# Fifteen tiles of each edge loop fetched row by row through SyncE's queue instead of gathered by GpSimd

## What is computed

```python
def layer0(x, src, dst, edge_attr, u, W1, b1, W2, b2):      # batch is all zeros
    all_feat = concatenate([x[dst], x[src], edge_attr, u[0] for each edge])
    msg = relu(all_feat @ W1 + b1)
    agg = segment_sum(msg, dst)
    return relu(concatenate([x, agg, u[0] for each node]) @ W2 + b2)
def layer1(h, fc_weight, attn_weight, src, dst, etype):
    Z = einsum('ni,rio->nro', h, fc_weight)                  # 8 relations
    z_s, z_d = Z[src, etype], Z[dst, etype]
    e = relu(sum(concatenate([z_s, z_d]) * attn_weight[etype]))
    alpha = softmax of e over the edges of each dst
    return segment_sum(alpha[:, None] * z_s, dst)
x = layernorm(x + layer0(...)); x = layernorm(x + layer1(...)); return x
```

## Time and profile before

| | |
|---|---|
| median of 3 runs | 4239.44 us |
| the profiled execution's own time | 4242.57 us |
| its span, first to last instruction | 4240.8 us |
| busy share of the span | PE 77%, PE weight loads 68%, DVE 70%, ACT 30%, POOL 72% |
| layer 0's gathers, on POOL | 36.1 to 1997.0 us |
| layer 1's gathers, on POOL | 2195.9 to 4156.1 us |
| mean granted TensorE clock | 0.519 |

### The profile page before, as it was taken

How to read it: one execution, slowest core, us unless ns; L and a number is a source line. 1 busy time by engine, 2 the same in 40 slices (tenths; PEclk the granted TensorE clock), 3 DMA queues, 4 the chain that set the end, 5 groups by cost and what they waited for, 6 DMA issues and landing times. The chain is left out here.

```text
span 4240.8 us, 71158 instructions
## 1 busy us (share of the span) xinstructions
PE 3261.1 (77%) x18045; PEld 2899.6 (68%) x18045; DVE 2980.9 (70%) x9475; ACT 1266.3 (30%) x4137; POOL 3036.0 (72%) x3266
## 2 busy tenths in 40 slices
PE   7867677777777777777857777787878888888884
PEld 6866666666676766767636666676767777777774
DVE  6867677777677777777446666676767777777777
ACT  3000000000000000000224545554555555555553
POOL 5777777777777777776147777777777777777774
PEclk7555555555555555555665555555555555555555
DMA  6322222222222222222352222222222222222221
GB/s 196 105 70 61 69 72 60 69 72 71 70 62 70 72 70 72 72 70 47 135 198 58 52 54 58 48 59 58 58 49 58 58 58 58 59 58 56 51 58 37
DMA packets 172567, 300.16 MB, mean 71 GB/s; under 512 B 71746, under 2 KB 78262, under 8 KB 158871
## 3 DMA queue, kind: packets, MB, share of 16 engines
q0 software_dynamic: 100032, 105.03, 14.8%
q1 hardware_dynamic: 70688, 188.26, 12.5%
q10 hardware_dynamic: 1462, 2.30, 0.2%
HBM read 260.37 MB, written 34.99 MB: 70 GB/s over the span
## 5 line engine op out<-in xcount | busy, mean ns | idle before, releaser
L451 POOL DMA_INDIRECT ring<-Btab,idx x1563 | 1484.7, 950 | 510.2 <-issue 443.7
L451 POOL DMA_INDIRECT ring<-Ztab,idx x1563 | 1485.2, 950 | 493.2 <-issue 449.5
L1312 PE MATMUL p_s<-ring,ohx 128*128 x3328 | 808.0, 421 | 122.7 <-issue 120.0
L1312 PEld LDWEIGHTS p_s<-ring,ohx 128*128 128x128 f32 x3328 | 735.8, 326 | 142.7 <-issue 142.7
L732 PEld LDWEIGHTS p_s<-msg,oh 128*128 128x128 f32 x3328 | 725.7, 331 | 101.8 <-issue 101.8
L732 PE MATMUL p_s<-msg,oh 128*128 128x64 f32 x3328 | 758.3, 423 | 47.4 <-ACT msg L632 44.1
L719 PE MATMUL p_m<-A,oht 128*128 x1664 | 436.7, 364 | 430.6 <-DVE full L853 423.0
L632 ACT ACTIVATE msg<-p_t 128x512 f32<-128x512 f32 x208 | 124.2, 597 | 1802.7 <-DVE p_t L859 1796.4
L719 PEld LDWEIGHTS p_m<-A,oht 128*128 128x128 bf16 x1664 | 234.6, 142 | 507.7 <-issue 462.3
L724 PE MATMUL p_m<-W1c,eaT 65*128 65x128 f32 x1664 | 572.6, 448 | 6.0 <-DMA eaT<-in_eaT_in 6.0
L1402 DVE SCALAR_TENSOR_TENSOR XA<-XA,ff,p_s 128x65 f32 x1664 | 467.5, 281 | 128.5 <-DVE XA L1402 70.5
(11 more groups left out here) (204 smaller groups left out, 3132.0 us busy)
## 6 DMA issues: line engine op xcount, KB each, us to landing
drow<-drow_d SPq DMA_DIRECT2D x104, 1024.0 KB
eaT<-in_eaT_in SPq DMA_DIRECT2D x208, 128.0 KB
Ztab<-Z_stage SPq DMA_DIRECT2D x49, 536.0 KB, 4.1
ring<-Btab,idx POOLq DMA_INDIRECT x1563
ring<-Ztab,idx POOLq DMA_INDIRECT x1563
xTB<-in_xTB_in SPq DMA_DIRECT2D x7, 448.0 KB, 7.0
Btab<-B_stage SPq DMA_DIRECT2D x7, 448.0 KB, 5.9
ring<-in_xTA_in SPq DMA_DIRECT2D x7, 448.0 KB, 6.3
```

Of the source, the lines that this page charges most:

```text
L451: e.indirect_dma_start(out=ring[:, t % RING, :], out_offset=None, in_=table[:, :], in_offset=bass.IndirectOffsetOnAxis(ap=idx[:, t:t + 1], ...
L1312: last = e.matmul(pS[s % 2][h][:, j % 4, :], OHx[:, s % 2, j, :], ring[:, bass.ds(t, 1), 0:D + 1], start=True, stop=True)
```

## The change

Of each edge loop, fifteen tiles are no longer gathered by POOL: the last tile of the super-tiles 17, 29, 41 and so on to 185 (`fetched_tile`). SP fetches each of them by 128 DMAs of one row each, eleven for each compute step, spread over twelve steps. It reads the row numbers from a small table in SBUF (`srow`), which it loads for one fetched tile ahead. The super-tiles that contain a fetched tile lie in 24 more places behind the ring (`place`). DVE works these places out in the input phase, with fifteen more small operations. POOL's `counted` waits for the fetched rows (`A.s_row`) beside the gathers of that super-tile. The tables of slot places lie in one SBUF tensor (`tabs`), so layer 1 does not load `xrow` a second time. In layer 1, SP waits for the phase's tables before it loads the first `drow`; before, two `drow` loads came ahead of that wait.

```diff
+W = 12
+SPARE = 3
+ROWS = -(-P // W)
+FIRST = W + 5
+NK = len(range(FIRST, TO - 1, W))
...
+            step, base = W * O, (FIRST - W) * O
+            done(e.tensor_scalar(out=lim[:, :, :], in0=A.iota[:, 0:16].unsqueeze(1), scalar1=float(step), scalar2=float(base), op0=ALU.mult, op1=ALU.add))
...
+            done(e.tensor_tensor(out=tm[:, :], in0=tm[:, :], in1=off[:, :], op=ALU.add))
+            for w in range(2):
+                done(e.tensor_copy(A.val[:, :, w, 2], tm[:, :]))
             e.wait_ge(s_pc, 1)
...
+def place(t):
...
+    s, j = divmod(t, O)
+    n, off = divmod(s - FIRST + W, W)
+    return RING + n % SPARE * O + j if off == 0 and n >= 0 else t % RING
...
+def fetched(e, A, s, ring, table, of, regs, used):
...
+    k, i = divmod(s, W)
+    if k >= NK:
+        return
+    t = fetched_tile(k)
+    if i == 0:
+        if k >= 2:
...
+            e.wait_ge(used, t // O - SPARE * W + BEHIND + 1)
+            e.wait_ge(A.s_row[k % 2], 16 * P * (k // 2))
+        e.wait_ge(A.s_srow, 16 * (k + 1))
+        if k + 1 < NK:
+            numbers(e, A, of, k + 1)
+    for p in range(i * ROWS, min((i + 1) * ROWS, P)):
+        if p % O == 0 or p == i * ROWS:
+            e.reg_load(regs, A.srow[0:1, k % 2 * P + p // O * O:k % 2 * P + p // O * O + O])
+        r = e.snap(regs[p % O], min_val=0, max_val=table.shape[0] - 1)
+        e.dma_start(ring[p:p + 1, place(t), :], table[bass.ds(r, 1), :]).then_inc(A.s_row[k % 2], 16)
...
-        e.indirect_dma_start(out=ring[:, t % RING, :], out_offset=None, in_=table[:, :],
-                             in_offset=bass.IndirectOffsetOnAxis(ap=idx[:, t:t + 1], axis=0)).then_inc(s_g[s % len(s_g)], 16)
+        if t not in others:
+            e.indirect_dma_start(out=ring[:, place(t), :], out_offset=None, in_=table[:, :],
+                                 in_offset=bass.IndirectOffsetOnAxis(ap=idx[:, t:t + 1], axis=0)).then_inc(s_g[s % len(s_g)], 16)
...
                     e.dma_start(eaT[0:2 * DE, s % QE, :, :], of[bass.ds(t, 1), :, :, :].rearrange("a f i k -> (a f) i k")).then_inc(s_ea[s % QE], 16)
+                    fetched(e, A, s, ring, A.Btab, src, regs, S["full"])
...
-            for g in range(SO // G):
-                rows_loaded(e, A, drow, s_dr, S["oht"], g)
-            e.wait_ge(s_ix, 80)
+            e.wait_ge(s_ix, 64)
+            numbers(e, A, A.ix1_d, 0)
+            regs = [e.alloc_register(f"l1sr{j}") for j in range(O)]
+            for s in range(SO):
+                if s % G == 0:
+                    rows_loaded(e, A, drow, s_dr, S["oht"], s // G)
+                fetched(e, A, s, ring, A.Ztab, A.ix1_d, regs, S["s"])
+            e.wait_ge(A.s_srow, 16 * NK)
```

More of the change, by code:

```diff
@@ L43 @@
 assert RT >= BEHIND + 5
+assert (SPARE - 1) * W > BEHIND and ROWS * W >= P and W > 6
 assert NS >= NT + NB - 1 and NS % P == 0 and TO % Q == 0 and SO % Q == 0 and SO % G == 0
@@ L129, in phase_inputs @@
         tm = sb("t_mod", [P, SC], F32)
+        lim = sb("t_lim", [P, 1, 16], F32)
+        ge = sb("t_ge", [P, SC, 16], F32)
+        tn = sb("t_n", [P, SC], F32)
+        off = sb("t_off", [P, SC], F32)
+        isn = sb("t_is", [P, SC], F32)
         pB = [[bank(ctx, nc, f"p_b{k}{h}", [P, QC, D]) for h in range(2)] for k in range(2)]
@@ L433, in weave, with fetched_tile, numbers @@
                 streams.remove(g)
+def place(t):
+    s, j = divmod(t, O)
+    n, off = divmod(s - FIRST + W, W)
+    return RING + n % SPARE * O + j if off == 0 and n >= 0 else t % RING
+def fetched_tile(k):
+    return (FIRST + k * W) * O + O - 1
+def numbers(e, A, of, k):
+    e.dma_start(A.srow[0:1, k % 2 * P:(k % 2 + 1) * P], of[:, fetched_tile(k):fetched_tile(k) + 1].rearrange("p c -> c p"),
+                allow_slow_non_contiguous=True).then_inc(A.s_srow, 16)
+def fetched(e, A, s, ring, table, of, regs, used):
[15 more added lines that the diff above has]
+        e.dma_start(ring[p:p + 1, place(t), :], table[bass.ds(r, 1), :]).then_inc(A.s_row[k % 2], 16)
 def gathers(e, A, ring, table, idx, s_g, landed, used, free={}):
+    others = {fetched_tile(k): k for k in range(NK)}
+    tiles = lambda s: sum(t < NT and t not in others for t in range(s * O, (s + 1) * O))
     def counted(s):
-        tiles = min(O, NT - s * O)
-        before = sum(min(O, NT - i * O) for i in range(s % len(s_g), s, len(s_g)))
-        e.wait_ge(s_g[s % len(s_g)], 16 * (before + tiles))
+        e.wait_ge(s_g[s % len(s_g)], 16 * sum(tiles(i) for i in range(s % len(s_g), s + 1, len(s_g))))
+        k = others.get(s * O + O - 1)
+        if k is not None:
+            e.wait_ge(A.s_row[k % 2], 16 * P * (k // 2 + 1))
         e.sem_inc(landed, 1)
@@ L524, in phase_layer0 @@
         s_io = sem("l0_io")
-        T = {n: sem("t_" + n) for n in ("dve count before middle low high typ val sq sel tab d0 rows rowt rowi back table dh dl lt yt ys "
-                                        "drow typd ixd ix a hi lo rem parts zero").split()}
+        T = {n: sem("t_" + n) for n in ("dve count before middle low high typ val sq sel tab d0 rows rowt rowi table dh dl lt yt ys "
+                                        "drow typd ix a hi lo rem parts zero").split()}
         block = ctx.enter_context(nc.Block())
@@ L531, in _ @@
             treg = e.alloc_register("l0st")
+            regs = [e.alloc_register(f"l0sr{j}") for j in range(O)]
             for i, (q0, q1) in enumerate(CHUNKS):
@@ L546, in _, with loads @@
             e.wait_ge(T["drow"], 16)
-            e.wait_ge(T["table"], 48)
+            e.wait_ge(T["table"], 64)
             rows_loaded(e, A, drow, s_dr, S["oht"], 0)
-            def loads(of):
+            def loads(of, src):
+                numbers(e, A, src, 0)
                 for s in range(SO):
@@ L1184, in _ @@
             e.wait_ge(A.s_x, 32)
+            for k in range(2):
+                take(e, A.s_row[k], 16 * P * len(range(k, NK, 2)))
+            take(e, A.s_srow, 16 * NK)
 def phase_layer1(nc, A):
@@ L1550, in build @@
         A.flag = sb("flag", [1, 1], I32)
-        A.brow = sb("brow", [1, NS], I32)
+        A.tabs = sb("tabs", [P, NS], I32)
+        A.brow = A.tabs[0:1, :]
+        A.wrow = A.tabs[32:33, :].rearrange("a (s j) -> a s j", j=O)
+        A.xrow = A.tabs[64:65, 0:SO * WX].rearrange("a (s w) -> a s w", w=WX)
+        A.srow = A.tabs[96:97, 0:2 * P]
+        A.s_row = [ctx.enter_context(nc.semaphore(f"rows_fetched{i}")) for i in range(2)]
+        A.s_srow = ctx.enter_context(nc.semaphore("row_numbers"))
         A.dstl = sb("dstl", [P, NS], BF16)
```

65 lines of the change are left out of this document (36 added, 29 removed).

## The result

| | before | after |
|---|---|---|
| median, same chip | 4239.44 us (4236.49 to 4252.38, 5 runs) | 4196.04 us (4194.93 to 4197.75, 5 runs) |
| profiled execution, its span | 4242.57, 4240.8 us | 4197.56, 4195.8 us |
| POOL busy | 3036.0 us | 3002.0 us |
| first gather to last, layer 0 | 1960.8 us | 1941.3 us |
| first gather to last, layer 1 | 1960.2 us | 1936.1 us |

The account below looks back on a forecast made before the run. POOL's gathers, 1.248 us each, were taken to bound both loops. Terms of -37.4 + 1.4 - 0.4 = -36.4 us took the median of 4239.44 to 4203.0 us; the forecast's own range was 4197 to 4212, with rival 3 to 4224.

Parts of the forecast that it names:

- What bounds the kernel: Both edge loops: POOL's indirect gathers set the pace, one every 1.248 us, 0.944 of making and 0.304 of queue.
- The main term: POOL in both loops: fifteen gathers fewer in each, 15 x 1.248 = 18.7 us, twice, 37.4 us saved.
- The changed names of semaphores and tables cost nothing: Closing part of the layer 1 start step: renamed semaphores and tables were put at no cost.
- the sum for everything but the gathers: Input phase +1.4 us and layer 1's start -0.4 us; all other terms were put at nothing.
- SP's queue: SP in both loops: rows 0.35 to 0.57 us each, eight-register loads 0.55; layer 0 step 5.8 to 8.2 us, costing nothing.
- the threshold of 0.68 us a row: SP in layer 0: row cost above which SP rather than POOL sets the pace, (9.34 - 2.1)/10.7.
- Whether the rows are in time: POOL's wait for fetched rows: they land about six super-tiles of 10 us ahead, so cost nothing.
- The input phase and layer 1's start: Ahead of the loops: DVE's fifteen more operations +1.4 us (0.5 to 2.5); layer 1 without the `xrow` load -0.4 us.
- 1, SP as the bound: SP's queue, both loops: dear rows make SP set the pace, about 4670 us at 0.87 us a row; chance 0.07.
- 2, rows in one engine's line: Row DMAs run one after another at 2.0 us, POOL waits for each fetched tile, about 8000 us; chance 0.02.
- 3, layer 0's gain eaten by late `eaT`: SP's queue in layer 0: row DMAs delay `eaT` past POOL's landing, 18.7 us lost, 4222 us; chance 0.06.
- 4, no effect: POOL waits for late rows about as long as a gather takes, 4240 us; chance 0.04.

Follow-up runs that it names:

- the kernel before with the longer form: Layer 1's OHT comparison as tensor_tensor with a broadcast operand instead of tensor_scalar, in the kernel before the change: 4296.07 us against 4242.31, ratio 1.0130.

## Why the prediction was right or wrong

**What bounds the kernel: right.** In both loops POOL, at 1.248 us a gather, before and after; DVE and PE waited for it in 153 and 119 steps where it had been 158 and 115.

**The main term: right.** 15 x 1.248 = 18.7 us a loop. Measured in layer 1 by itself 18.6 us, in layer 0 19 to 20 in the traces and 15 to 17 in the medians.

**The step that failed: "The changed names of semaphores and tables cost nothing", a term put at nothing, and with it the sum for everything but the gathers,** which was +1.4 - 0.4 = +1.0 us. Measured without fetched tiles it was -6.1 us (-9 to -2), and this difference of 7 us is about what the forecast was off by, 43.4 for 36.4; the range had no room for it, as none of its bounds was for the loops without the tiles. The reason given for the term was in effect that PE has time, and a search for what such a change costs finds nothing. It brought a gain: in the traces 4.6 us of layer 1's gathers, 1960.2 to 1955.6, since fewer of DVE's `OHT` comparisons fell ahead of a gather and held it up (51 long ones became 31). I had read 80 gathers in 100 us as 1.248 us each, and not looked at the few that took longer, though the earlier trace rows has the maximum of 1.21 us. That a comparison holds up a gather is shown by two runs and by the records. What moved the comparisons stays open: the tables in the shared tile made two of PE's loads 0.18 us longer, which fits, but the run that puts the loads back did not fall in a session paced by POOL. The -2.8 us between the layers is no part of the change: in the sessions of the same kind the other runs had 160.8 to 164.4 us there, the kernel before with the longer form 162.5, and the 166.5 before is one execution's.

**SP's queue: the answer right, its parts off.** A row is 0.225 us of issue and 0.42 with its register operations, inside 0.35 to 0.57; a load of eight registers is 0.78 behind rows instead of 0.55, `xrow`'s 0.54 instead of 0.27. In all SP is occupied for 7.4 us a step without `drow` (5.8 to 8.2 forecast) against POOL's 9.34. The room was smaller than the threshold of 0.68 us a row says: without its rows a step has 7.4 - 10.7 x 0.42 = 2.9 us on SP instead of 2.1, which leaves (9.34 - 2.9) / 10.7 = 0.60 us.

**Whether the rows are in time: right.** 1.5 us of waits, five times.

**The input phase and layer 1's start: right.** +1.5 us for +1.4; -0.3 for -0.4.

**The rivals.** 1, SP as the bound: not where the forecast was measured, but it is what happens with each row fetched twice, and in the sessions of 5630 to 5660 us, where the change is slower by 3.2%. I had given it one cause, a dear row; it has another, pauses between instructions. 2, rows in one engine's line: refuted, as POOL never waited for a fetched tile for more than a part of those 1.5 us. The Trainium skill's rule on what k an SP copy runs on (DMA: Bandwidth & Descriptors, section Why a DMA increments its semaphore by 16 and not by 1) cost this kernel nothing that a run shows. As the prediction read it, layer 0's rows would be cut up over 16 engines; the packet records have each fetched row in one piece, 1920 packets of 256 bytes more than without the tiles in layer 0 and 1920 of 268 bytes, 16 ns each, in layer 1. 3, layer 0's gain eaten by late `eaT`: 26.1 us of PE waits in 12 steps, and layer 0's loop lost nothing by them. 4, no effect: refuted.

## What to carry to other kernels

Where one engine's issue sets the pace, work moved to a queue that is waiting anyway brings what the issue time says (18.6 us in layer 1's traces for 18.7 forecast); the queue's room is to be counted with everything that it issues, register loads too, and it runs out suddenly: against a pace of 9.3 us, 7.4 us a step were free, 8.8 brought part of what they should, and 11 cost 382 us. What has time to spare can still matter by when it runs, as DVE's comparison and POOL's gathers show; a count of those instructions that take longer than the median finds that, and a row of minimum and median hides it. And a gain that rests on thousands of additional instructions should be measured in more than one session: this one is 1.1% in one kind and a loss of 3.2% in the other.

## What the runs showed of the hardware

- DVE's comparisons with their tensors in SBUF and GpSimd's indirect DMAs hold each other up. A gather of 0.944 us took 1.19 beside a 0.48 us comparison begun 0.10 us ahead of it and 1.80 beside one of 1.22 us begun 0.23 us ahead: 0.944 us and what was left of the comparison 0.13 us behind the gather's start. In layer 1, before and after the change, all comparisons that made a gather of over 1.0 us began 0.29 to 0.08 us ahead of it or 0.40 to 0.47 us behind its start. Begun 0.48 to 0.70 us behind it, the comparison took up to 0.70 us and the gather 0.94. A comparison of 1.22 us with one operand in PSUM did nothing, in 60 cases.
- On PE, a register load took 305 ns for one value from a tile of its own and 484 from partition 64 of a shared tile; 590 and 769 for eight values from partition 32. The load of `trow` right behind the one of `brow` stayed at 592. On SP, a load of one value from partition 64 took 276 ns, and 538 behind row transfers. Why, no run tells.
- A DMA of one row of 64 or 67 floats, its address from a register, took SP 0.22 to 0.23 us of issue and 0.42 us from one to the next, and was one packet.
- The same kernel on the same chip took 5660 us in one session and 4243 in the next, with the same median duration of a layer 0 matmul (0.421 us) and of a gather (0.944 us) and, on PE and SP, pauses of about 2 us between instructions that waited for nothing.
